# Attention with chosen places: who forms the sum of each head's 32 found values

## The chip, the cores and the metric

One Trainium2 chip, one of its cores. The metric is the device time of one execution in microseconds (us). Three runs of the kernel before gave 1508.18, 1509.52 and 1509.85; the median is 1509.52.

## The reference, cut to what matters

The model has four layers of gated cross-attention and feed-forward over 64 sequences of 64 tokens of 128 features. The change touches one sublayer, the attention of layer 1. It attends with only the 32 best of 64 context places for each token and head (4 heads of 32 features):

```
scores = einsum('bthd,bghd->bhtg', Q, K) / sqrt(DH)
topv, topi = top_k(scores, 32)
probs = softmax(topv)
attn = zeros_like(scores).at[bi, hi, ti, topi].set(probs)
attn_mean = attn.mean(axis=1)
c_t = einsum('btg,bgd->btd', attn_mean, x_vision @ Wv)
```

The result c_t gives scales and shifts (FiLM) for a state-space layer that comes after. The sum in the softmax runs over the 32 chosen places only.

## The kernel before

The 4096 tokens are 32 tiles of 128 tokens, tokens on partitions. The sublayer is `attention_ssm`. Each engine runs its own written list of steps, one step per tile (`pe_step`, `act_step`, `dve_step`, `pool_step`), and semaphores hold them together. The order in each step is written out by hand, and each queue is worked strictly in order. ScalarE and TensorE run their middle steps in a loop of two tiles each, VectorE and POOL only from tile 16 on.

**VectorE**, step t. For tiles 2 to 14 it first adds two tiles of the routed experts' rows, which POOL has gathered (`route.dve_pair`). Then it finds the 32 largest scores of each head in four rounds (`topk_round`): in each round four `max` (L1986) give the eight largest of each head, into `m8`, and four `match_replace` (L1992) overwrite them in the scores with the value TAKEN. After the first round it forms `nm`, the negative scaled maximum (L1995). Norm work for later tiles lies between the rounds. At the end it multiplies the exponentials `EX` with "was taken" (L2041), which zeroes the places that were not chosen, sums each head over its 64 places (L2043), and takes the reciprocal (L2045). The semaphore `tk` counts the halves of the rounds, 16 for each tile.

**ScalarE**, step t (`act_step`), in this order: scores of tile t+1 out of PSUM (L2161); values of t (L2170); `act_scale` of tile t-1, which waits for the reciprocal, masks it (L2151) and scales the four heads of EX (L2154); the norm's transpose and the keys of tile t+2 (L2175, L2133); the transposed attention of t-1 (L2179); the exponentials of tile t, 4 of 128x64 (L2182), which wait for `nm`; the context of t-1 (L2186); the query of t+2 (L2139); a norm of t+3 (L2146); the FiLM rows of t-1 (`act_film`, L2198 and L2199), which wait for TensorE's product.

**TensorE**, step t: scores of t+1 (L2270), values of t, transpose and keys of t+2, the bias row of the FiLM product of t-1 (L2291), then the transposed attention of t-1 (L2278, waits for act_scale), its context (L2286), the query of t+2 (L2262) and the FiLM product of t-1 (L2295, waits for L2186).

**POOL**, step t: the context mask onto the scores of t+1 (L1869), norm steps for later tiles, the modulation with the FiLM rows of t-1 (L1833, L1836), and in steps 0 to 12 the gathers of routed rows (L1316).

`thr_hits`, a scratch of 128 x 2 x 1032 bf16, belongs to another part of the kernel that counts weights above a threshold while layer 0 runs; in this sublayer it is free.

Of the kernel before, what the change touches and what calls it, by code (L numbers as in the profile page):

```python
# [11 lines left out]
ALU = mybir.AluOpType  # L12
ACT = mybir.ActivationFunctionType
AX = mybir.AxisListType
F32 = mybir.dt.float32
# [8 lines left out]
TILES = TOK // P  # L24
# [1682 lines left out]
def attention_ssm(k, io, freed, route):  # L1707


    nc = k.nc  # L1710
    H, DH, KTOP, GATE, HID = 4, 32, 32, 1, 4
    SCALE = float(DH) ** -0.5
    MASKED, TAKEN = -1e38, -3e38
    sem = lambda n, total=TILES: k.sem("a1_" + n, total)
# [4 lines left out]
    cv = Carve(k.arena)  # L1719
# [23 lines left out]
    W = cv.f32(2, H, CTX)  # L1743
    W2 = cv.f32(2, H, CTX)
    EX = cv.f32(2, H, CTX)
    m8 = cv.f32(4, H, 8)
    nm, sums, rec = cv.f32(2, H), cv.f32(2, H), cv.f32(2, H)
    vs = cv.f32(2, 2, D)
    aT = cv.f32(2, P)
# [13 lines left out]
    xt_full, xt_laid, q_full, q_laid, k_full, k_laid = (sem(n) for n in ("xT_full", "xT_laid", "q_full", "q_laid", "k_full", "k_laid"))  # L1763
    s_full, s_laid, s_masked, v_full, v_laid = (sem(n) for n in ("scores", "scores_laid", "masked", "v_full", "v_laid"))
    tk = sem("top", 16 * TILES)
    e_done, sel_done, n_step, a_done = sem("exp"), sem("selected"), sem("norm_step", 2 * TILES), sem("attn")
    r_done = sem("recip_masked")
    a_full, a_laid, c_full, cT_laid, f_full, f_laid = (sem(n) for n in ("attnT_full", "attnT_laid", "cT_full", "cT_laid", "film_full", "film_laid"))
    xs_step, xs_done = sem("xs_step"), sem("xs_done")

# [11 lines left out]
    def flat(v):  # L1782
        return v.rearrange("p h j -> p (h j)")

    def more(t, ahead):
        return not isinstance(t, int) or t + ahead < TILES
# [188 lines left out]
    def topk_round(e, t, s, r):  # L1975


        V = nc.vector
        src = W if r == 0 else W2
        before_round = 16 * t + 4 * r  # L1980
        for half in range(2):
            if r > 0:
                e.wait_ge(tk.sem, tk.at(before_round - 1 + half))
                e.nop(nofuse=True)
            for h in (2 * half, 2 * half + 1):
                ins = V.max(m8[:, r, h, :], src[:, s, h, :])  # L1986
            ins.then_inc(tk.sem, 1)
        for half in range(2):
            e.wait_ge(tk.sem, tk.at(before_round + 1 + half))
            e.nop(nofuse=True)  # L1990
            for h in (2 * half, 2 * half + 1):
                ins = V.match_replace(W2[:, s, h, :], m8[:, r, h, :], src[:, s, h, :], TAKEN)  # L1992
            ins.then_inc(tk.sem, 1)
        if r == 0:
            V.tensor_scalar(nm[:, s, :], m8[:, 0, :, 0], -SCALE, None, ALU.mult).then_inc(nm_done.sem, 1)  # L1995

    def norm_a(e, t, s):
        e.wait_ge(ln_rstd_done.sem, ln_rstd_done.at(t + 1))
        e.nop(nofuse=True)
        nc.vector.tensor_scalar(k.xn[:, s, 0, :], k.x[:, t, :], k.mv[:, 0, s, 0:1], k.rstd[:, 0, s:s + 1],  # L2000
                                ALU.subtract, ALU.mult).then_inc(ln_out_done.sem, 1)

    nm_done = sem("max_laid")

    def stats_a(e, t, s):
        nc.vector.bn_stats(k.stat[:, 0, s, :], k.x[:, t, :]).then_inc(ln_stats_done.sem, 1)

    def aggregate_a(e, t, s):
        e.wait_ge(ln_stats_done.sem, ln_stats_done.at(t + 1))
        e.nop(nofuse=True)  # L2010
        nc.vector.bn_aggr(k.mv[:, 0, s, :], k.stat[:, 0, s, :]).then_inc(ln_mv_done.sem, 1)

    def dve_step(e, t, s):

        V = nc.vector
        o = 1 - s
        if isinstance(t, int) and 2 <= t < 2 + route.PAIRS:
            route.dve_pair(e, t - 2)
        e.wait_ge(s_masked.sem, s_masked.at(t + 1))
        e.nop(nofuse=True)  # L2020
        topk_round(e, t, s, 0)
        if isinstance(t, int) and 2 <= t < 16:
            e.wait_ge(before.sem, min(route.AHEAD + 2 * t - 2, TILES))
            e.nop(nofuse=True)
        if more(t, 4):
            stats_a(e, t + 4, s)
        topk_round(e, t, s, 1)
        if more(t, 3):
            e.wait_ge(u_kept.sem, u_kept.at(t + 2))
            e.nop(nofuse=True)  # L2030
            e.wait_ge(xt_full.sem, xt_full.at(t + 2))
            e.wait_ge(b_out.sem, b_out.at(t + 2))
            norm_a(e, t + 3, o)
        topk_round(e, t, s, 2)
        if more(t, 4):
            aggregate_a(e, t + 4, s)
        topk_round(e, t, s, 3)
        e.wait_ge(e_done.sem, e_done.at(t + 1))
        e.wait_ge(tk.sem, tk.at(16 * t + 16))

        V.scalar_tensor_tensor(flat(EX[:, s, :, :]), flat(W2[:, s, :, :]), TAKEN, flat(EX[:, s, :, :]), ALU.is_equal, ALU.mult).then_inc(sel_done.sem, 1)  # L2041
        e.wait_ge(sel_done.sem, sel_done.at(t + 1))
        V.tensor_reduce(sums[:, s, :], EX[:, s, :, :], AX.X, ALU.add).then_inc(n_step.sem, 1)  # L2043
        e.wait_ge(n_step.sem, n_step.at(2 * t + 1))
        V.reciprocal(rec[:, s, :], sums[:, s, :]).then_inc(n_step.sem, 1)  # L2045

    def dve_first(e):
# [81 lines left out]
    def act_keys(e, t, s):  # L2129

        e.wait_ge(k_full.sem, k_full.at(t + 1))
        for h in range(H):
            last = nc.scalar.activation(kbd[:, s, :, h, :], ps[:, 2, 0:P].rearrange("p (b j) -> p b j", b=2), ACT.Copy,  # L2133
                                        scale=head_of[:, h:h + 1])
        last.then_inc(k_laid.sem, 1)

    def act_query(e, t, s):
        e.wait_ge(q_full.sem, q_full.at(t + 1))
        nc.scalar.copy(qT[:, s, :], ps[:, 1, 0:P]).then_inc(q_laid.sem, 1)  # L2139

    def act_norm_u(e, t, s):

        e.wait_ge(ln_out_done.sem, ln_out_done.at(t + 1))
        e.wait_ge(b_rstd.sem, b_rstd.at(t + 1))
        e.nop(nofuse=True)
        nc.scalar.activation(XS[:, t, :], k.xn[:, s, 0, :], ACT.Copy, scale=k.rstd[:, 1, s:s + 1]).then_inc(b_out.sem, 1)  # L2146

    def act_scale(e, t, s):

        e.wait_ge(n_step.sem, n_step.at(2 * t + 2))  # L2150
        nc.scalar.activation(rec[:, s, :], rec[:, s, :], ACT.Copy, scale=tmask[:, t:t + 1] if isinstance(t, int) else tmask[:, bass.ts(t, 1)]).then_inc(r_done.sem, 1)  # L2151
        e.wait_ge(r_done.sem, r_done.at(t + 1))
        for h in range(H):
            last = nc.scalar.activation(EX[:, s, h, :], EX[:, s, h, :], ACT.Copy, scale=rec[:, s, h:h + 1])  # L2154
        last.then_inc(a_done.sem, 1)

    def act_scores(e, t, s):
        e.wait_ge(s_full.sem, s_full.at(t + 1))
        if not (isinstance(t, int) and t < 2):
            e.wait_ge(tk.sem, tk.at(16 * t - 28))  # L2160
        nc.scalar.copy(flat(W[:, s, :, :]), ps[:, 3, 0:H * CTX]).then_inc(s_laid.sem, 1)  # L2161

    def act_step(e, t, s):

        o = 1 - s
        film = not (isinstance(t, int) and t == 0)
        if more(t, 1):
            act_scores(e, t + 1, o)
        e.wait_ge(v_full.sem, v_full.at(t + 1))
        nc.scalar.copy(vs[0:CTX, s, :, :].rearrange("p b d -> p (b d)"), ps[0:CTX, 4, 0:2 * D]).then_inc(v_laid.sem, 1)  # L2170
        if film:
            act_scale(e, t - 1, o)
        if more(t, 2):
            e.wait_ge(xt_full.sem, xt_full.at(t + 3))
            nc.scalar.copy(k.xnT[:, s, 0:P], ps[:, 0, 0:P]).then_inc(xt_laid.sem, 1)  # L2175
            act_keys(e, t + 2, s)
        if film:
            e.wait_ge(a_full.sem, a_full.at(t))
            nc.scalar.copy(aT[0:CTX, o, :], ps[0:CTX, 5, 0:P]).then_inc(a_laid.sem, 1)  # L2179
        e.wait_ge(nm_done.sem, nm_done.at(t + 1))  # L2180
        for h in range(H):
            last = nc.scalar.activation(EX[:, s, h, :], W[:, s, h, :], ACT.Exp, bias=nm[:, s, h:h + 1], scale=SCALE)  # L2182
        last.then_inc(e_done.sem, 1)
        if film:
            e.wait_ge(c_full.sem, c_full.at(t))
            nc.scalar.copy(cT[:, o, :], ps[:, 6, 0:P]).then_inc(cT_laid.sem, 1)  # L2186
        if more(t, 2):
            act_query(e, t + 2, s)
        if more(t, 3):
            act_norm_u(e, t + 3, o)  # L2190
        if film:
            act_film(e, t - 1, o)

    def act_film(e, t, s):
        e.wait_ge(xs_done.sem, xs_done.at(t))
        e.wait_ge(f_full.sem, f_full.at(t + 1))
        e.nop(nofuse=True)
        nc.scalar.copy(F[:, s, :], ps[:, 7, 0:2 * D])  # L2198
        nc.scalar.copy(FO[:, t, :], ps[:, 7, 2 * D:4 * D]).then_inc(f_laid.sem, 1)  # L2199
# [1147 lines left out]
```

## Time and profile before

| | us |
|---|---|
| median of three runs | 1509.52 |
| profiled execution, its own time | 1522.08 |
| span of its trace | 1520.4 |
| VectorE busy (share of the span) | 1090.0 (72%) |
| ScalarE busy | 922.1 (61%) |
| POOL busy | 687.8 (45%) |
| TensorE matmul busy | 1343.0 (88%) |
| this sublayer's tile loop | about 481 to 740 |

The profile is one execution, and its own time is above the median of the runs. A timeline row has the start, the duration (of all instructions merged in it), engine, line, operation, output and input, count, and in brackets the idle time of the engine before it with what ended it. "issue" is idle time for which the profile shows no cause. The granted clock of TensorE (PEclk) is a share of its full speed, 1.0.

### The profile page before, as it was taken

How to read it: one execution, taken by the hardware profiler on the slowest of the kernel's cores; microseconds unless marked ns; L12 is line 12 of the kernel's file. 1: busy time of each engine (PE TensorE's matmuls, PEld its weight loads, DVE VectorE, ACT ScalarE, POOL GpSimd, SP SyncE). 2: the span in 40 equal slices, each digit the busy share in tenths (PEclk: the TensorE clock that was granted, in tenths of full speed). 3: DMA queues.
4: the chain of work that ended last, by engine and by line, in shares of the span. 5: the costliest groups of instructions: out<-in, count | busy, mean ns of one | idle time of the engine just before them, and what ended most of it. 6: DMA issues, size and time to landing. Idle time of an engine off the chain costs nothing.

```text
span 1520.4 us, 49785 instructions
## 1 busy us (share of the span) xinstructions
PE 1343.0 (88%) x17625; PEld 1029.3 (68%) x17657; DVE 1090.0 (72%) x4573; ACT 922.1 (61%) x2012; POOL 687.8 (45%) x1336
## 2 busy tenths in 40 slices
PE   6999999999658688887789599988999999999998
PEld 5888888877545344444556366666877777788885
DVE  5878788877424799999868544436899899766664
ACT  5666665655335577787233355545688889865553
POOL 3655555576434688766166211113443343343331
PEclk9999999999875888899989799998999999999999
DMA  8050000001455401000020100000000000000000
GB/s 186 3 123 0 0 0 2 5 29 34 124 168 134 96 18 29 1 0 1 16 52 0 36 1 0 0 1 2 3 2 0 0 2 3 3 9 7 7 15 22
DMA packets 66868, 43.05 MB, mean 28 GB/s; under 512 B 24597, under 2 KB 63210, under 8 KB 66602
## 3 DMA queue, kind: packets, MB, share of 16 engines
q1 hardware_dynamic: 58346, 33.89, 9.1%
q0 software_dynamic: 2048, 4.20, 1.0%
q10 hardware_dynamic: 6336, 3.15, 0.7%
q8 instruction: 83, 1.36, 0.4%
q14 instruction: 55, 0.45, 0.1%
HBM read 28.64 MB, written 12.58 MB: 27 GB/s over the span
## 4 chain that ended last, share of the span: by engine, by line
PE 60%; DVE 18%; issue 8%; ACT 6%; POOL 5%; DMA 2%; DVEq 1%; SPq 0%; POOLq 0%; ACTq 0%
PE ps L775 4%; PE ps L344 4%; PE ps L784 4%; DVE arena L1992 4%; PE ps L386 4%; PE ps L337 4%; PE ps L366 3%; PE ps L2723 3%; DVE arena L1986 3%; PE ps L2730 3%; PE ps L377 3%; PE ps L2804 3%; PE ps L357 2%; PE ps L2717 2%; PE ps L2773 2%
## 5 line engine op out<-in xcount | busy, mean ns | idle before, releaser
L3236 POOL TENSOR_TENSOR arena<-arena 128x512 f32<-128x512 f32 x64 | 67.8, 1059 | 112.6 <-DVE arena L3160 112.6
L1992 DVE MATCH_REPLACE8 arena<-arena 128x64 f32<-128x64 f32 x512 | 101.8, 209 | 0.5 <-issue 0.2
L2482 DVE TENSOR_SCALAR_CACHE_REDUCE thr_hits<-thr_abs,thr_candidate 128x512 bf16<-128x512 f32 (+1 forms) x248 | 101.8, 477 | 0.0
L2723 PE MATMUL ps<-arena,toeplitz 96*128 96x128 f32 x512 | 71.5, 283 | 9.2 <-ACT arena L2955 4.0
L668 POOL TENSOR_TENSOR ln_veps<-ln_mv,eps 128x4 f32<-128x4 f32 x32 | 9.1, 284 | 154.5 <-DVE ln_mv L662 154.5
L1986 DVE MAX8 arena<-arena 128x8 f32<-128x64 f32 x512 | 75.9, 210 | 3.3 <-issue 2.0
L616 POOL TENSOR_TENSOR arena<-arena 128x1024 f32<-128x1024 f32 x32 | 61.4, 1918 | 34.8 <-DVE arena L557 34.8
L538 DVE TENSOR_REDUCE arena<-ps 128x16 f32<-128x1024 f32 x32 | 39.1, 1223 | 52.9 <-PE ps L357 52.8
L784 PEld LDWEIGHTS ps<-arena,toeplitz 128*128 128x128 f32 x512 | 63.5, 192 | 16.0 <-issue 13.3
L386 PEld LDWEIGHTS ps<-arena 128*64 128x64 f32 x1024 | 60.2, 139 | 19.8 <-issue 11.4
L2723 PEld LDWEIGHTS ps<-arena,toeplitz 96*128 96x128 f32 x512 | 63.0, 193 | 15.0 <-ACT arena L2955 9.8
L2717 PE MATMUL ps<-xnT,toeplitz 128*128 128x128 f32 x512 | 69.9, 281 | 3.2 <-ACT xnT L2894 3.2
L2804 PE MATMUL ps<-arena 128*64 128x128 f32 x1024 | 67.8, 273 | 3.1 <-ACT arena L2906 3.1
L2730 PE MATMUL ps<-toeplitz,arena 96*64 96x256 f32 x512 | 70.3, 396 | 0.0
L2804 PEld LDWEIGHTS ps<-arena 128*64 128x64 f32 x1024 | 59.9, 136 | 14.8 <-ACT arena L2906 7.0
L775 PE MATMUL ps<-xnT,arena 128*128 128x512 f32 x128 | 67.8, 622 | 0.0
L3134 DVE TENSOR_REDUCE arena<-ps 128x8 f32<-128x512 f32 x64 | 43.9, 685 | 33.4 <-PE ps L2792 33.3
L2278 PEld LDWEIGHTS ps<-ident,arena 128*64 128x64 f32 x256 | 28.0, 140 | 57.9 <-ACT arena L2154 56.4
L2717 PEld LDWEIGHTS ps<-xnT,toeplitz 128*128 128x128 f32 x512 | 63.8, 196 | 4.2 <-ACT xnT L2894 4.1
L386 PE MATMUL ps<-arena 128*64 128x128 f32 x1024 | 64.0, 277 | 2.1 <-ACT arena L457 2.1
L344 PE MATMUL ps<-xnT,arena 128*128 128x128 f32 x512 | 64.3, 280 | 1.6 <-DVE x_res L529 0.6
L784 PE MATMUL ps<-arena,toeplitz 128*128 128x128 f32 x512 | 64.9, 274 | 0.0
(463 smaller groups left out, 4157.2 us busy)
## 6 DMA issues: line engine op xcount, KB each, us to landing
toeplitz<-ssm_toeplitz_scratch SPq DMA_DIRECT2D x2, 2048.0 KB
arena<-L_ffn_packed SPq DMA_DIRECT2D x24, 128.5 KB, 3.2
toeplitz<-L_ffn_packed SPq DMA_DIRECT2D x24, 128.5 KB, 2.2
f_rows<-arena SPq DMA_DIRECT2D x2, 1536.0 KB, 9.5
f_outs<-arena ACTq DMA_DIRECT2D x12, 256.0 KB, 2.7
ssm_toeplitz_scratch<-ssm_padded_kernel SPq DMA_DIRECT2D x1, 2048.0 KB
out<-x_res SPq DMA_DIRECT2D x8, 256.0 KB, 2.3
arena<-ctx SPq DMA_DIRECT2D x2, 768.0 KB, 5.8
```

The lines of the kernel that those rows point to most:

```text
L344: last = nc.tensor.matmul(ps[:, 2 + c // 4, c % 4 * P:(c % 4 + 1) * P], w_q[:, c * P:(c + 1) * P], k.xnT[:, s, 0:P], start=True, stop=True)
L386: last = nc.tensor.matmul(ps[64 * b:64 * b + 64, 2, 0:D], OT[:, b, c, :], w_o[:, b, c, :], start=(c == 0), stop=(c == C - 1))
L775: nc.tensor.matmul(ps[:, u % 3, :], w1[:, x, c * P:(c + 1) * P], xnT, start=True, stop=True).then_inc(h_full.sem, 1)
L784: last = nc.tensor.matmul(ps[:, 3 + x % 2, j * P:(j + 1) * P], hT[:, u % 3, j * P:(j + 1) * P], w2[:, x, c, :], start=(c == 0 and j == 0), ...
L1986: ins = V.max(m8[:, r, h, :], src[:, s, h, :])
L1992: ins = V.match_replace(W2[:, s, h, :], m8[:, r, h, :], src[:, s, h, :], TAKEN)
L2482: ins = V.tensor_scalar(self.hits[:, j, at:at + n], self.abs[:, at:at + n], self.cand[:, c:c + 1].bitcast(F32), 0.0, ALU.is_ge, ALU.add, a ...
L2717: last = T_.matmul(ps[:, 1, c * P:(c + 1) * P], weights[phase].q[:, c * P:(c + 1) * P], xnT[:, s * P:(s + 1) * P], start=True, stop=True)
L2723: last = T_.matmul(ps[:, 0, c * P:(c + 1) * P], weights[phase].k[0:DC, c * P:(c + 1) * P], cg[0:DC, s, :], start=True, stop=True)
L2730: last = T_.matmul(ps[64 * m:64 * m + 64, 5, 256 * b:256 * b + 256], cg[0:DC, s, b * CTX:(b + 1) * CTX], by_parity[0:DC, m, :, :], start=T ...
L2804: last = T_.matmul(ps[64 * m:64 * m + 64, 0, 0:D], OT[:, m, c, :], w_o[:, m, c, :], start=(c == 0), stop=(c == C - 1))
L3236: G_.tensor_tensor(probs, probs, rc[:, s, :].unsqueeze(2).to_broadcast([P, heads, CTX]), ALU.mult).then_inc(s_prob.sem, 1)
```

## The change

The 32 found values of a tile stand in `m8` after the fourth search. Before, only the current tile's were kept, laid out by round. Now they are kept for two tiles in turn in `thr_hits`, so that each head's 32 values form a list. ScalarE takes the exponential of each head's list with an accumulated output, which is the head's sum (`act_sums`). It does so at the end of its step, after the FiLM rows, and waits for the fourth search's `max` only (`tk` at 14 of 16). VectorE drops its own sum and waits for ScalarE's before the reciprocal. `act_scale` waits for the selection by itself.

```diff
-    m8 = cv.f32(4, H, 8)
+    cv.at += 4 * H * 8
+    spare = k.thresholds.hits[:].rearrange("p a b -> p (a b)").bitcast(F32)
+    m8 = spare[:, 0:2 * H * 32].rearrange("p (s h r j) -> p s r h j", s=2, r=4, h=H)
+    top = spare[:, 256:256 + H * 32].rearrange("p (h j) -> p h j", h=H)
+    m8_list = spare[:, 0:2 * H * 32].rearrange("p (s h j) -> p s h j", s=2, h=H)
...
-                ins = V.max(m8[:, r, h, :], src[:, s, h, :])
+                ins = V.max(m8[:, s, r, h, :], src[:, s, h, :])
...
         V.scalar_tensor_tensor(flat(EX[:, s, :, :]), flat(W2[:, s, :, :]), TAKEN, flat(EX[:, s, :, :]), ALU.is_equal, ALU.mult).then_inc(sel_done.sem, 1)
-        e.wait_ge(sel_done.sem, sel_done.at(t + 1))
-        V.tensor_reduce(sums[:, s, :], EX[:, s, :, :], AX.X, ALU.add).then_inc(n_step.sem, 1)
-        e.wait_ge(n_step.sem, n_step.at(2 * t + 1))
+        e.wait_ge(sum_done.sem, sum_done.at(t + 1))
         V.reciprocal(rec[:, s, :], sums[:, s, :]).then_inc(n_step.sem, 1)
...
     def act_scale(e, t, s):
-        e.wait_ge(n_step.sem, n_step.at(2 * t + 2))
+        e.wait_ge(n_step.sem, n_step.at(t + 1))
...
         e.wait_ge(r_done.sem, r_done.at(t + 1))
+        e.wait_ge(sel_done.sem, sel_done.at(t + 1))
...
         if film:
             act_film(e, t - 1, o)
+        act_sums(e, t, s)
+
+    def act_sums(e, t, s):
+        e.wait_ge(tk.sem, tk.at(16 * t + 14))
+        for h in range(H):
+            last = nc.scalar.activation(top[:, h, :], m8_list[:, s, h, :], ACT.Exp, bias=nm[:, s, h:h + 1], scale=SCALE, accum_out=sums[:, s, h:h + 1])
+        last.then_inc(sum_done.sem, 1)
```

## Rows read from the trace of the kernel before

**Rows 1.** The chain of waits over 478 to 742 us, shares by line.

```profile
by line: DVE arena L1992 21.0%; DVE arena L1986 17.1%; issue 17.1%; DMA arena<-f_outs,arena 6.5%; DVE arena L2041 3.5%; DVE arena L2043 3.4%; POOL arena L1316 3.3%; POOL arena L1869 2.7%; POOL ln_rstd L1827 1.6%; POOL ln_rstd L1853 1.5%; PO
```

**Rows 2.** Windows: stretch, its length, each engine's busy us, granted clock, DMA share, GB/s.

```profile
560.00:600.00 40.00, 30.59 (x141) 17.89 (x139) 36.57 (x273) 29.05 (x108) 34.00 (x74) 0.88 0.06 16
...
640.00:680.00 40.00, 31.51 (x155) 17.60 (x153) 38.22 (x295) 32.01 (x120) 28.91 (x73) 0.96 0.00 0
```

**Rows 3.** Timeline of VectorE: the reciprocals of tiles 3, 14, 27 and 31.

```profile
522.02 0.18 DVE L2045 RECIPROCAL arena<-arena 128x4 f32<-128x4 f32 x1
...
611.20 0.18 DVE L2045 RECIPROCAL arena<-arena 128x4 f32<-128x4 f32 x1
...
706.61 0.18 DVE L2045 RECIPROCAL arena<-arena 128x4 f32<-128x4 f32 x1
...
733.65 0.18 DVE L2045 RECIPROCAL arena<-arena 128x4 f32<-128x4 f32 x1
```

**Rows 4.** Timeline of POOL: two starts of its step.

```profile
567.78 0.98 POOL L1869 TENSOR_TENSOR arena<-arena 128x256 f32<-128x256 f32 x1
...
576.18 0.98 POOL L1869 TENSOR_TENSOR arena<-arena 128x256 f32<-128x256 f32 x1
```

**Rows 5.** Timeline of ScalarE over one tile, from 626.89 us.

```profile
626.89 0.30 ACT L2151 ACTIVATE arena<-arena 128x4 f32<-128x4 f32 x1
...
629.63 1.07 ACT L2182 ACTIVATE arena<-arena 128x64 f32<-128x64 f32 x4
...
632.10 0.37 ACT L2198 COPY arena<-ps 128x256 f32<-128x256 f32 x1 [0.43 <-PE ps L2295]
632.37 0.38 ACT L2199 COPY arena<-ps 128x256 f32 x1
632.74 0.37 ACT L2161 COPY arena<-ps 128x256 f32<-128x256 f32 x1
...
633.34 0.30 ACT L2151 ACTIVATE arena<-arena 128x4 f32<-128x4 f32 x1
```

**Rows 6.** Timeline of VectorE at the end of a tile: fourth search, selection, reciprocal.

```profile
653.32 0.57 DVE L1986 MAX8 arena<-arena 128x8 f32<-128x64 f32 x4
...
654.70 0.42 DVE L2041 SCALAR_TENSOR_TENSOR arena<-arena 128x256 f32<-128x256 f32 x1
...
655.61 0.18 DVE L2045 RECIPROCAL arena<-arena 128x4 f32<-128x4 f32 x1
```

**Rows 7.** A line of VectorE in layer 0: count, duration min/median/max in ns.

```profile
L2482 DVE DVE_READ_ACCUMULATOR thr_hits<-thr_abs,thr_candidate x248: 75/84/90, 29.2 to 373.4; 128x1 f32 x124
```

**Rows 8.** ScalarE's groups by line and shape: busy us, mean ns of one, idle before.

```profile
L2182 ACT ACTIVATE arena<-arena 128x64 f32<-128x64 f32 x128 | 34.1, 339 | 8.4 <-DVE arena L1995 8.4
L2936 ACT ACTIVATE arena<-arena 128x512 f32<-128x512 f32 x64 | 40.4, 632 | 3.9 <-DVE arena L3138 2.7
L1229 ACT COPY arena<-ps 128x8 f32 x16 | 2.9, 183 | 0.0
```

**Rows 9.** Timeline of ScalarE: from act_scale to the first FiLM copy in three tiles.

```profile
545.30 0.30 ACT L2151 ACTIVATE arena<-arena 128x4 f32<-128x4 f32 x1
...
550.50 0.37 ACT L2198 COPY arena<-ps 128x256 f32<-128x256 f32 x1 [0.43 <-PE ps L2295]
...
594.39 0.30 ACT L2151 ACTIVATE arena<-arena 128x4 f32<-128x4 f32 x1 [2.01 <-DVE arena L2045]
...
600.77 0.37 ACT L2198 COPY arena<-ps 128x256 f32<-128x256 f32 x1 [1.03 <-PE ps L2295]
...
692.22 0.30 ACT L2151 ACTIVATE arena<-arena 128x4 f32<-128x4 f32 x1 [0.31 <-DVE arena L2045]
...
697.42 0.37 ACT L2198 COPY arena<-ps 128x256 f32<-128x256 f32 x1 [0.47 <-PE ps L2295]
```

**Rows 10.** Timeline of ScalarE in the last tiles.

```profile
727.45 0.30 ACT L2151 ACTIVATE arena<-arena 128x4 f32<-128x4 f32 x1 [0.47 <-DVE arena L2045]
...
732.93 0.38 ACT L2199 COPY arena<-ps 128x256 f32<-128x256 f32 x1
```

More of the change, by code:

```diff
@@ L1765, in attention_ssm @@
     tk = sem("top", 16 * TILES)
-    e_done, sel_done, n_step, a_done = sem("exp"), sem("selected"), sem("norm_step", 2 * TILES), sem("attn")
-    r_done = sem("recip_masked")
+    e_done, sel_done, n_step, a_done = sem("exp"), sem("selected"), sem("recip"), sem("attn")
+    r_done, sum_done = sem("recip_masked"), sem("top_sums")
     a_full, a_laid, c_full, cT_laid, f_full, f_laid = (sem(n) for n in ("attnT_full", "attnT_laid", "cT_full", "cT_laid", "film_full", "film_laid"))
@@ L1991, in topk_round @@
             for h in (2 * half, 2 * half + 1):
-                ins = V.match_replace(W2[:, s, h, :], m8[:, r, h, :], src[:, s, h, :], TAKEN)
+                ins = V.match_replace(W2[:, s, h, :], m8[:, s, r, h, :], src[:, s, h, :], TAKEN)
             ins.then_inc(tk.sem, 1)
         if r == 0:
-            V.tensor_scalar(nm[:, s, :], m8[:, 0, :, 0], -SCALE, None, ALU.mult).then_inc(nm_done.sem, 1)
+            V.tensor_scalar(nm[:, s, :], m8[:, s, 0, :, 0], -SCALE, None, ALU.mult).then_inc(nm_done.sem, 1)
     def norm_a(e, t, s):
```

## The prediction, made before the result was known

> **What bounds the kernel now.** I went first to the chain of waits over the stretch in which the attention with chosen places runs, 478 to 742 us. There the reader sees that VectorE carries most of it: the match-and-replace line 21.0%, the search for the eight largest 17.1%, the selection 3.5% and the row sum 3.4%, with some POOL lines behind [rows 1]. Then the windows: at 640 to 680 VectorE is busy 38.22 of 40 us, ScalarE 32.01, POOL 28.91; at 560 to 600 VectorE 36.57, POOL 34.00, ScalarE 29.05 [rows 2]. By shares ScalarE has about 8 us in 40 to spare. The timelines decide where that room lies.
>
> The starts of the reciprocal, one per tile, give the pace. Tile 3 is at 522.02, tile 14 at 611.20, tile 27 at 706.61 and tile 31, the last, at 733.65 [rows 3]. That is 8.11 us a tile for 11 tiles, 7.34 for 13 and 6.76 for 4. In the first of these POOL, which also gathers the routed rows, goes round in 8.40 us (576.18 less 567.78) without waiting [rows 4], and late in the stretch VectorE is held to it. From tile 15 on VectorE sets the pace alone.
>
> Now ScalarE. From 626.89 to 633.34 it was behind and waited for no reciprocal: one whole tile takes it 6.45 us [rows 5]. Of these, 5.21 pass from the masking of the reciprocal (L2151) to the first film copy (L2198), 0.64 on the two film copies, and 0.60 on the scores and values copies (L2161, L2170). It is 6.45 and not less because the queue waits inside it for TensorE, which waits for ScalarE's own earlier results (the 0.43 at L2198). So the queue's own round is 6.45 us against 7.34, a slack of 0.89 and not the 1.5 that the shares suggest.
>
> **The change part by part.** VectorE loses the row sum. From the start of the selection to that of the reciprocal are 0.91 us (655.61 less 654.70), of which the selection is 0.42 and 0.03 for the handover [rows 6]; the sum with its own handover is the other 0.46. All of it lies on VectorE's own path, so with nothing else it would be worth 0.46 in each tile that VectorE paces. Which memory holds the list, and the stride, change no instruction's count; I cost them at nothing, by the same size of operand. The moved wait for the selection in act_scale costs nothing either: the selection ends before the sums do, below.
>
> ScalarE gains four exponentials of 128x32 with an accumulated output, last in its step, behind the film copies. Call their time in the queue S. Four exponentials of 128x64 take 1.07 us [rows 5], and one of them 339 ns [rows 8], so they start (1.07 - 0.34)/3 = 0.24 apart. Half the columns are worth little: (632 - 339)/448 is 0.65 ns a column, 0.02 for 32, which leaves 0.22 each and 0.87 for four. The accumulated output on ScalarE stands nowhere in this trace. On VectorE it is an instruction of its own, DVE_READ_ACCUMULATOR, 84 ns [rows 7]. I bound it from below by nothing (S = 0.87), from above by a full loss of the overlap and a read as long as ScalarE's own shortest copy: 0.32 + 0.18 = 0.50 each [rows 8], S = 2.0. A gain below 0.87 is excluded, since the four are added whole and nothing leaves this queue. I take half the overlap lost and a read like VectorE's, the one row of such a read: 0.22 + 0.05 + 0.08 = 0.35, S = 1.4.
>
> The Trainium skill (ScalarE: Activation LUTs, Rules for kernel authors) budgets about 0.3 us for an ACTIVATE with a pointer bias and 0.83 ns an element, by which S would be 1.3. For four of 64 columns it gives 1.4 where the trace shows 1.07; the trace decides for plain ones, and for accumulating ones no row speaks. By the rule the sum below would be some 3 us smaller.
>
> What is queued behind decides. The reciprocal of tile t now waits for sums(t). Sums(t) stand behind film(t-1), and that stands behind act_scale(t-1), which waits for the reciprocal of t-1. So a ring closes that was open before: reciprocal, mask and scale, TensorE's transposes, the copy, exponentials of tile t, context, film product, film copies, sums, reciprocal. After the sums ScalarE does the scores and values copies (0.60), and under them the reciprocal (0.18 [rows 6]) is done. The ring's period is 6.45 + S. VectorE waits in it: its fourth search ends at 653.89 [rows 6], 6.1 us behind the reciprocal before it, and sums begin 6.45 behind it (0.60 + 5.21 + 0.64), so the wait on the search costs nothing and the sums end after the selection in every tile.
>
> Third, TensorE. The 5.21 is at full clock. Over the seven tiles whose L2151 starts at 545.30 to 594.39 the same way takes 5.20, 6.15, 5.20, 7.40, 5.21, 5.21 and 6.38: the last is 600.77 less 594.39 [rows 9]. That is 0.61 over 5.21 in the mean, in a stretch with TensorE busy 30.59 of 40 us and a granted clock of 0.88, both of its levels by turns; for the ten from 626.89 to 692.22 it is 0.09 (one at 0.85), at a clock of 0.96 [rows 2, 5, 9]. Call it K. Before, K hardly cost anything, for the reciprocal set the next start; in the ring it counts in full. The new ring idles TensorE by S more in each tile, like the first stretch; I take K = 0.45, nearer to it, bounds 0.09 and 0.61.
>
> The period is then 6.45 + 1.4 + 0.45 = 8.30. POOL's 8.40 of the first stretch is hardly touched: it is ahead of VectorE there and waits for nothing. But VectorE ran at less than that up to tile 8 and built up the lead that it lost later, and now it goes at 8.30 from tile 3 on. From tile 3 to 27: 24 x 8.30 = 199.2 against 184.6, +14.6. For the last four tiles keys, queries and scores fall away and TensorE fills the gaps: 727.45 to 732.93 is 5.48, plus 0.37 (633.34's tile, 632.37 to 632.74) is 5.85 to the sums [rows 5, 10]; then S, the reciprocal with two handovers 0.33, and K of 0.2 since these tiles all ran at full clock: 7.78 x 4 = 31.1 against 27.0, +4.1. Tiles 0 to 2 are hidden: VectorE waits there for gathered rows, and the film copies on which those hang come ahead of the added work. What follows the loop is untouched.
>
> Sum: +18.7 us. On the profiled execution, 1522.08 us (span 1520.4 and 1.7 around it), this is 1540.8. The median of the runs is 12.6 us below that execution; I carry the difference over: 1528.2 us.
>
> At the low ends (S 0.87, K 0.09) the period is 7.41: POOL still hides the first 11 tiles, 13 x 7.41 is +0.9, the tail +1.2: +2, 1511.6. At the high ends (2.0, 0.61) it is 9.06: 217.4 - 184.6 = +32.8, and the tail is 4 x 8.79 less 27.0 = +8.1: +41, 1550.5.
>
> **The rivals.** First, the sums are hidden and the row sum's time comes back. Mechanism: ScalarE gets to the sums before VectorE's selection ends, so the reciprocal waits for nothing. For it speaks ScalarE's idle time, 2.01 us in front of a single L2151 [rows 9]. Against it: that idle time lies in front of act_scale, behind the reciprocal, and the ring has none of it. It decides where 6.45 + S + K is under VectorE's new round of 7.34 - 0.46 = 6.88, thus S + K under 0.43, or if the queue's round is shorter than I read. It would give 0.46 x 17 tiles (15 to 31) = -7.8: 1501.7 us. Chance 0.07.
>
> Second, the ring closes but S and K are at their low ends and POOL covers the early tiles: +0 to +3, 1511 us. Chance 0.10.
>
> Third, a read of the accumulator that stops the queue, and a TensorE that falls to its lower level in every tile, K about 1 instead of by turns. With S at 1.7: 9.15 x 24 = 219.6, +35.0, and the tail 4 x 8.88 less 27.0 = +8.5: 1553. For it speaks the 7.40 in the middle of the first stretch; against it that four of its seven tiles were at full clock. Chance 0.15.
>
> **How the numbers follow.** My forecast, between +4 and +30, has the remaining 0.68; its time, 1528.2, is the predicted one. The range for 8 in 10 runs from the low ends to just under the third rival's sum: 1511 to 1547. A difference of over 0.2%, 3 us, is about what a measurement of this kernel tells from none. Faster takes the first rival, 0.07. Within it lies most of the second, 0.09. Slower is the rest, 0.84.
>
> **What would show it.** In the profile after, TENSOR_REDUCE is gone from the loop and the reciprocal is preceded by idle VectorE time of 1 us or more, ended by ScalarE's exponentials; ScalarE no longer waits for the reciprocal in front of act_scale, only for TensorE; the reciprocals are 8.3 us apart from tile 3 to 27 and 7.8 in the last four. The exponentials of 128x32 with their reads show S directly: 1.4 us for four. The granted clock between 600 and 720 falls from 0.96 toward 0.88. It would be wrong if the reciprocal follows the selection without idle time (first rival), or if the period is right while S and K are not: then the ring is right and its terms are mis-sized.

## The result and the profile after

The changed kernel took 1516.84 us (median of 7 runs, 1514.09 to 1522.02) against 1509.85 for the kernel before beside it (7 runs): ratio 1.0046, 95% interval 1.0027 to 1.0066, so +6.9 us with 4 to 10. Slower, as forecast, but by little more than a third of the +18.7.

The two profiled executions stand the other way round: 1514.1 us of span against 1520.4. That difference lies ahead of this sublayer. Part of it can be seen: in the execution of before, TensorE stood still once for 13.59 us in the routed experts of layer 0, on its timeline:

```profile
427.42 1.86 PE L1360 MATMUL ps<-arena 128*128 128x128 f32 x7 [13.59 <-issue]
```

The changed kernel's execution has no such gap there; its longest between 400 and 480 us is 7.99 us, and it reaches tile 3 fourteen us earlier. The gap is of the execution and not of the change: e2 and e10 below are one and the same kernel and show 14.71 and 7.03 us. So I count from the reciprocal of tile 3 to the end of the span: 1520.4 - 522.0 = 998.4 before, 1514.1 - 507.9 = 1006.2 after, +7.8, which agrees with the runs. The reciprocals that answer to [rows 3], from VectorE's timeline of the changed kernel:

```profile
507.93 0.18 DVE L2047 RECIPROCAL arena<-arena 128x4 f32<-128x4 f32 x1 [0.57 <-ACT thr_hits L2201]
...
595.42 0.18 DVE L2047 RECIPROCAL arena<-arena 128x4 f32<-128x4 f32 x1 [0.45 <-ACT thr_hits L2201]
...
695.38 0.18 DVE L2047 RECIPROCAL arena<-arena 128x4 f32<-128x4 f32 x1 [0.94 <-ACT thr_hits L2201]
...
726.07 0.18 DVE L2047 RECIPROCAL arena<-arena 128x4 f32<-128x4 f32 x1 [1.40 <-ACT thr_hits L2201]
```

| us | tiles 3 to 14 (11) | 14 to 27 (13) | 27 to 31 (4) | sum |
|---|---|---|---|---|
| before | 89.2 | 95.4 | 27.0 | 211.6 |
| after | 87.5 | 100.0 | 30.7 | 218.1 |
| forecast for after | 91.3 | 107.9 | 31.1 | 230.3 |

Of the 32 reciprocals 27, and all from tile 14 on, now have idle VectorE time in front of them, ended by ScalarE's exponentials. From the waits of VectorE over 478 to 740 us (total, times, longest), and the windows that answer to [rows 2]:

```profile
DVE arena L2047 <- ACT thr_hits L2201: 25.2, 27, 2.2
```

```profile
560.00:600.00 40.00, 30.86 (x146) 17.14 (x145) 35.52 (x283) 34.23 (x150) 34.35 (x77) 0.91 0.11 27
640.00:680.00 40.00, 31.40 (x149) 17.38 (x147) 33.37 (x274) 35.26 (x158) 27.04 (x70) 0.92 0.00 0
```

At 640 to 680 VectorE fell from 38.2 to 33.4 busy us and ScalarE rose from 32.0 to 35.3. One tile of ScalarE, from its timeline; it answers to [rows 5] and shows the new work (L2201), with the second and third head left out:

```profile
626.73 0.31 ACT L2153 ACTIVATE arena<-arena 128x4 f32<-128x4 f32 x1
...
631.94 0.37 ACT L2208 COPY arena<-ps 128x256 f32<-128x256 f32 x1 [0.42 <-PE ps L2305]
632.21 0.38 ACT L2209 COPY arena<-ps 128x256 f32 x1
632.47 0.33 ACT L2201 ACTIVATE thr_hits<-thr_hits,arena 128x32 f32<-128x32 f32 x1
632.70 0.20 ACT L2201 ACTIVATION_READ_ACCUMULATOR thr_hits<-thr_hits,arena 128x1 f32 x1
...
633.40 0.31 ACT L2201 ACTIVATE thr_hits<-thr_hits,arena 128x32 f32<-128x32 f32 x1
633.61 0.19 ACT L2201 ACTIVATION_READ_ACCUMULATOR thr_hits<-thr_hits,arena 128x1 f32 x1
633.70 0.36 ACT L2164 COPY arena<-ps 128x256 f32<-128x256 f32 x1
633.95 0.37 ACT L2173 COPY arena<-ps 64x256 f32<-64x256 f32 x1
634.22 0.31 ACT L2153 ACTIVATE arena<-arena 128x4 f32<-128x4 f32 x1
```

The way from L2153 to L2208 is still 5.21 us. S is 1.23 (632.47 to 633.70), and the whole tile 7.49. On VectorE, the selection ends at 632.92 and the reciprocal follows 0.93 us later, which answers to [rows 6]:

```profile
632.49 0.43 DVE L2045 SCALAR_TENSOR_TENSOR arena<-arena 128x256 f32<-128x256 f32 x1
633.84 0.18 DVE L2047 RECIPROCAL arena<-arena 128x4 f32<-128x4 f32 x1 [0.93 <-ACT thr_hits L2201]
```

Most tiles are 7.49 us apart. About every third or fourth takes 8.3 to 8.5, and in these TensorE's FiLM product takes 2.08 us where it takes 1.13 in the next tile, at a mean granted clock of 0.80 against 1.00: for part of the tile TensorE is at the lower of its two levels, 1.2 GHz, and for the rest at 2.4. ScalarE's timeline, TensorE's, and windows over the two tiles:

```profile
618.28 0.31 ACT L2153 ACTIVATE arena<-arena 128x4 f32<-128x4 f32 x1
...
624.45 0.37 ACT L2208 COPY arena<-ps 128x256 f32<-128x256 f32 x1 [1.32 <-PE ps L2305]
```

```profile
619.74 1.09 PE L2288 MATMUL ps<-ident,arena 128*64 128x128 f32 x8 [1.46 <-ACT arena L2157]
...
622.29 2.08 PE L2305 MATMUL ps<-arena 128*128 128x512 f32 x2
...
630.73 1.13 PE L2305 MATMUL ps<-arena 128*128 128x512 f32 x2
```

```profile
618.30:624.50 6.20, 4.37 (x18) 2.36 (x20) 5.99 (x52) 4.62 (x20) 3.61 (x10) 0.80 0.00 0
626.70:632.00 5.30, 3.94 (x20) 2.15 (x20) 5.30 (x48) 4.67 (x20) 3.03 (x8) 1.00 0.00 0
```

### The profile page after: what moved, and what is told of

Read it like the earlier page. It is cut to its first block, busy times and chain, and to the rows that moved or that the text cites. A ratio compares the mean times of both kernels' runs of the same rounds, so it can differ in the third digit from the quotient of the medians.

```text
span 1514.1 us, 50106 instructions
## 1 busy us (share of the span) xinstructions
PE 1331.0 (88%) x17657; PEld 1019.0 (67%) x17657; DVE 1073.0 (71%) x4541; ACT 953.6 (63%) x2268; POOL 687.7 (45%) x1336
## 4 chain that ended last, share of the span: by engine, by line
PE 34%; DVE 7%; ACT 5%; issue 3%; POOL 2%; DVEq 0%; ACTq 0%; POOLq 0%
PE ps L775 4%; PE ps L784 4%; PE ps L2733 3%; PE ps L2740 3%; PE ps L2814 3%; PE ps L2727 2%; PE ps L2783 2%; PE ps L2794 2%; PE ps L2886 2%; PE ps L2802 2%; PE ps L2855 1%; PE ps L2372 1%; PE ps L2395 1%; PE ps L2388 1%; POOL ln_rstd L670 1%
## 5 line engine op out<-in xcount | busy, mean ns | idle before, releaser
L1996 DVE MATCH_REPLACE8 arena<-thr_hits,arena 128x64 f32<-128x64 f32 x512 | 101.4, 208 | 0.0
L1990 DVE MAX8 thr_hits<-arena 128x8 f32<-128x64 f32 x512 | 75.7, 208 | 2.9 <-issue 1.9
L2288 PE MATMUL ps<-ident,arena 128*64 128x128 f32 x256 | 35.6, 283 | 39.8 <-ACT arena L2157 39.8
L2814 PE MATMUL ps<-arena 128*64 128x128 f32 x1024 | 67.8, 273 | 3.1 <-ACT arena L2916 3.1
L337 PE MATMUL ps<-arena 96*128 96x128 f32 x512 | 65.2, 281 | 0.0
```

The lines of the kernel that those rows point to most:

```text
L337: last = nc.tensor.matmul(ps[:, c // 4, c % 4 * P:(c % 4 + 1) * P], w_k[0:DC, c * P:(c + 1) * P], cg[0:DC, s, :], start=True, stop=True)
L1990: ins = V.max(m8[:, s, r, h, :], src[:, s, h, :])
L1996: ins = V.match_replace(W2[:, s, h, :], m8[:, s, r, h, :], src[:, s, h, :], TAKEN)
L2288: last = T.matmul(ps[0:CTX, 5, 0:P], EX[:, s, h, :], k.ident[:], start=(h == 0), stop=(h == H - 1))
L2814: last = T_.matmul(ps[64 * m:64 * m + 64, 0, 0:D], OT[:, m, c, :], w_o[:, m, c, :], start=(c == 0), stop=(c == C - 1))
```

## The experiments

Ten runs, each in five rounds against the kernel before on the same chip; e6 repeats the changed kernel and e10 repeats e2. The stretches are from one profiled execution each, as in the table above. "us" is the ratio less 1, times the median of before.

| kernel | ratio, interval | us | 3 to 14 | 14 to 27 | 27 to 31 |
|---|---|---|---|---|---|
| e1 sums unused, VectorE's sum kept | 1.0076, 1.0053 to 1.0099 | +11.6 | 89.1 | 99.4 | 30.6 |
| e2 sums ahead of the FiLM rows | 0.9981, 0.9964 to 0.9998 | -2.9 | 88.2 | 93.9 | 25.8 |
| e3 no sums at all | 0.9947, 0.9924 to 0.9969 | -8.1 | 88.4 | 87.8 | 25.3 |
| e4 filler of 384 columns | 1.0055, 1.0032 to 1.0078 | +8.4 | 88.2 | 101.1 | 30.4 |
| e5 no accumulated output | 1.0025, 1.0007 to 1.0044 | +3.8 | 87.7 | 96.0 | 30.8 |
| e6 changed kernel again | 1.0048, 1.0026 to 1.0069 | +7.3 | 87.7 | 102.5 | 30.7 |
| e7 e2 and the mask on VectorE | 1.0022, 1.0003 to 1.0041 | +3.3 | 89.1 | 96.6 | 26.4 |
| e8 filler of 640 columns | 1.0054, 1.0035 to 1.0073 | +8.2 | 87.6 | 97.5 | 29.8 |
| e9 e2 with the wait in halves | 0.9971, 0.9951 to 0.9991 | -4.4 | 88.1 | 91.8 | 25.5 |
| e10 e2 again | 0.9980, 0.9965 to 0.9995 | -3.0 | 88.6 | 92.3 | 25.8 |

The theory in the expectations: the time was lost because ScalarE's round of one tile became longer than VectorE's (queue theory). Its rival: it was lost because VectorE stands still for the sums (wait theory).

**e1.** Onto the changed kernel:

```diff
-        e.wait_ge(sum_done.sem, sum_done.at(t + 1))
+        e.wait_ge(sel_done.sem, sel_done.at(t + 1))
+        V.tensor_reduce(sums[:, s, :], EX[:, s, :, :], AX.X, ALU.add).then_inc(n_step.sem, 1)
+        e.wait_ge(n_step.sem, n_step.at(2 * t + 1))
         V.reciprocal(rec[:, s, :], sums[:, s, :]).then_inc(n_step.sem, 1)
...
-... accum_out=sums[:, s, h:h + 1])
+... accum_out=other[:, s, h:h + 1])
```

VectorE also waits at a step's start until the sums of two tiles before are done, since they read the same buffer; they are long done by then.

> ScalarE does its four accumulating exponentials as in the changed kernel, but their result goes to a tile that nobody reads; VectorE keeps its own row sum and never waits for them. Queue theory (the cost is that ScalarE's round of one tile, 6.26 us and the 1.23 us of the sums, is longer than the 7.34 us at which VectorE went): the wait of VectorE does not matter, so tiles 7.49 us apart with a jump now and then, and +5 to +8 us against before, like the changed kernel. Wait theory (the cost comes from VectorE standing still for the sums): the time of before, within 2 us.

Measured: +11.6 us, 99.4 in the 13 tiles. VectorE needs nothing of the new work and is held all the same, now in front of its selection, because the tile's own exponentials of 64 columns (L2189 here) come late from the same queue. Its timeline:

```profile
649.79 0.43 DVE L2047 SCALAR_TENSOR_TENSOR arena<-arena 128x256 f32<-128x256 f32 x1 [1.01 <-ACT arena L2189]
...
657.29 0.43 DVE L2047 SCALAR_TENSOR_TENSOR arena<-arena 128x256 f32<-128x256 f32 x1 [0.39 <-ACT arena L2189]
```

The wait theory falls. The idle time in front of the changed kernel's reciprocal is where the queue's length shows, not its cause. The size was outside the 5 to 8 us that I expected. The loop from tile 3 to 31 took 219.0 us, 7.4 more than before, as the queue theory has it. Another 3.3 come behind it: at the last reciprocal ScalarE still has its sums ahead of it, act_scale starts 2.22 us behind it (0.22 before), and the last tile's FiLM rows start 9.61 us behind it (6.28 before). The other 1.3 are TensorE's products at its lower level, as in the changed kernel.

**e2.**

```diff
+        act_sums(e, t, s)
         if film:
             act_film(e, t - 1, o)
-        act_sums(e, t, s)
```

> The changed kernel with the sums ahead of the FiLM rows in ScalarE's step. Queue theory with its order: the 0.42 us in which ScalarE waits for TensorE's FiLM product are now filled, so its round falls from 7.49 to about 7.1 and VectorE, at 6.88 in the mean, is nearly the pace: 1 to 5 us under before. If only the amount of work on ScalarE counts and not its place: the time of the changed kernel, +5 to +8.

Measured: -2.9 us, and 9.8 less than the changed kernel by the ratios. Nothing was taken away, only moved. The sums fill the time in which ScalarE waited for TensorE, so the FiLM copy has no idle time before it, and the tile is 6.96 us (ScalarE's timeline, 652.69 to 659.65). A second thing changes with the order: only one of the 13 tiles is a long one, at 8.01, where the changed kernel had three; the shorter tile is the larger part of the gain (13 times 7.49 less 7.13 is 4.7 of 6.1 us).

```profile
652.69 0.31 ACT L2153 ACTIVATE arena<-arena 128x4 f32<-128x4 f32 x1
...
657.08 0.40 ACT L2148 ACTIVATE arena<-xn,ln_rstd 128x128 f32 x1
657.39 0.30 ACT L2201 ACTIVATE thr_hits<-thr_hits,arena 128x32 f32<-128x32 f32 x1
...
658.61 0.35 ACT L2208 COPY arena<-ps 128x256 f32<-128x256 f32 x1
...
659.65 0.31 ACT L2153 ACTIVATE arena<-arena 128x4 f32<-128x4 f32 x1
```

**e3.** The four exponentials are replaced by one copy; the sums are left out and the result is not the attention's.

```diff
-        for h in range(H):
-            last = nc.scalar.activation(top[:, h, :], ..., accum_out=sums[:, s, h:h + 1])
-        last.then_inc(sum_done.sem, 1)
+        nc.scalar.copy(sums[:, s, :], k.onesq[:, 0:H]).then_inc(sum_done.sem, 1)
```

> Leaves the sums out: one ScalarE copy of 128x4 constants stands in their place, everything else as in the changed kernel. It shows what dropping VectorE's row sum is worth when ScalarE has no work for it. Queue theory: ScalarE's round is 6.26 and 0.2, VectorE paces at about 6.88: -5 to -8 us against before. If VectorE's row sum was not on the path: no gain.

Measured: -8.1 us, at the edge of the 5 to 8 expected. Tiles are 6.50 and 6.95 us apart by turns, and in most the reciprocal follows the selection with no wait (VectorE's timeline). This is what dropping the row sum is worth where ScalarE's share is free:

```profile
656.99 0.42 DVE L2045 SCALAR_TENSOR_TENSOR arena<-arena 128x256 f32<-128x256 f32 x1
657.33 0.17 DVE L2047 RECIPROCAL arena<-arena 128x4 f32<-128x4 f32 x1
657.42 0.58 DVE L1990 MAX8 thr_hits<-arena 128x8 f32<-128x64 f32 x4
...
663.83 0.17 DVE L2047 RECIPROCAL arena<-arena 128x4 f32<-128x4 f32 x1
...
670.78 0.17 DVE L2047 RECIPROCAL arena<-arena 128x4 f32<-128x4 f32 x1
```

**e4 and e8.** TensorE's wait for act_scale filled with unused products; e8's text is this, e4 has the first of the two only.

```diff
             pe_film_bias(e, t - 1)
+            for width in (BANK - P, 2 * P):
+                T.matmul(ps[:, 6, P:P + width], k.ident[:], wf[:, 0:width], start=True, stop=True)
             pe_attn(e, t - 1, o)
```

> The changed kernel with one more TensorE product (128x384, result unused) ahead of the transposed attention of each tile, where TensorE waits for ScalarE. Clock theory (tiles of 8.4 instead of 7.49 us are those where TensorE fell to its lower level in that wait): the long tiles go, 2 to 5 us less than the changed kernel, +2 to +5 against before. If the long tiles come from something else: the time of the changed kernel or more, and 8.4 us tiles stay.

> The changed kernel with TensorE's wait for act_scale filled by 640 columns of unused products instead of 384 as in e4. If the fall of the granted clock in every third or fourth tile comes from TensorE's idle time in that wait, it goes now or becomes rarer. If it does not depend on that idle time, tiles of 8.4 us stay as often as in e4, and the time is that of e4.

Measured: with 384 columns the long tiles stayed (four of 8.3 to 8.5 between tiles 14 and 27) and the time was that of the changed kernel, a miss. With 640 columns they are gone: all 13 tiles are 7.49 to 7.54 apart, and the granted clock at 640 to 680 is 1.00 against 0.92. The windows of e4 and of e8:

```profile
640.00:680.00 40.00, 34.57 (x158) 19.36 (x157) 33.67 (x276) 35.10 (x156) 27.06 (x71) 0.92 0.00 0
```

```profile
640.00:680.00 40.00, 35.95 (x179) 21.30 (x178) 36.20 (x294) 36.28 (x158) 26.16 (x68) 1.00 0.00 0
```

TensorE's wait for act_scale shows what the filler left of it. Outside the tiles next to a long one it is 1.46 us in the changed kernel and in e6 (three and four long tiles in the 13), 0.81 in e4 (four), 0.71 in e2 and e10 (one and none) and 0.38 in e8 (none). From TensorE's timelines of e4, e10 and e8:

```profile
659.03 1.09 PE L2288 MATMUL ps<-ident,arena 128*64 128x128 f32 x8 [0.81 <-ACT arena L2157]
```

```profile
657.18 1.09 PE L2288 MATMUL ps<-ident,arena 128*64 128x128 f32 x8 [0.71 <-ACT arena L2157]
```

```profile
653.03 1.09 PE L2288 MATMUL ps<-ident,arena 128*64 128x128 f32 x8 [0.38 <-ACT arena L2157]
```

So the long tiles come from TensorE's idle time, as far as one execution of each kernel shows it. But e8's runs did not become faster than e6's beside them (+8.2 and +7.3, intervals overlapping), though its 13 tiles took 5.0 us less than e6's in the profiled executions. The profiled execution of e8 was the fastest of its runs (1510.99 against a median of 1517.48) and that of e6 the slowest of its own (1522.38 against 1519.13), so these two may not stand for the rest; what the long tiles cost the runs is not shown. Part of it is that e8's last stretch, from ScalarE's first copy behind the convolution to the end of the span, was 765.4 us against 762.8. The executions fall into two groups there: before, after, e1, e6 and e10 at 762.8 to 763.2, e2, e3, e4, e5, e7, e8 and e9 at 765.4 to 767.2. Since e2 (766.0) and e10 (763.0) are the same kernel, the group belongs to the execution and not to the kernel.

**e5.** The four exponentials without their accumulated output, then the copy of e3; the result is not the attention's.

> The changed kernel with the four exponentials kept and the accumulated output left out; the sums are a 128x4 copy of constants, so the result is not the attention's. It splits S. If the accumulator's read costs queue time (starts 0.31 us apart with it against 0.22 without, as the traces show): 4 x 0.09 less and about 0.15 to 0.2 more for the copy, so tiles 7.3 us apart instead of 7.49, about 3 us under the changed kernel. If the read is free: the changed kernel's tile and 0.15 us more.

Measured: +3.8, 3.5 less than e6 beside it, with intervals that overlap; tiles are 7.22 us apart where TensorE's clock does not fall. ScalarE's timeline, four exponentials merged:

```profile
640.78 0.96 ACT L2201 ACTIVATE thr_hits<-thr_hits,arena 128x32 f32<-128x32 f32 x4
641.64 0.18 ACT L2202 COPY arena<-ones_square 128x4 f32<-128x4 f32 x1
```

Without the read four take 0.86 us of the queue (640.78 to 641.64), with it 1.23: the read costs 0.09 each, though it lasts 0.19, because it overlaps its neighbours.

**e6.** The changed kernel again.

> The changed kernel itself, on the chip and beside the kernels of this call. +5 to +10 us against before, the tile loop as in its first profile: 7.49 us a tile, with a long tile now and then.

Measured: +7.3 us. Its 13 tiles took 102.5 against 100.0, with three of 8.4 and one of 9.73 among them where the first had three: that much differs from execution to execution.

**e7.** On top of e2:

```diff
-        V.reciprocal(rec[:, s, :], sums[:, s, :]).then_inc(n_step.sem, 1)
+        V.reciprocal(rec[:, s, :], sums[:, s, :]).then_inc(r_done.sem, 1)
+        e.wait_ge(r_done.sem, r_done.at(t + 1))
+        V.tensor_scalar(rec[:, s, :], rec[:, s, :], tmask[...], None, ALU.mult).then_inc(n_step.sem, 1)
...
-        nc.scalar.activation(rec[:, s, :], rec[:, s, :], ACT.Copy, scale=tmask[...]).then_inc(r_done.sem, 1)
```

> The sums ahead of the FiLM rows as in e2, and the masking of the reciprocal (a 128x4 multiply) moved from ScalarE to VectorE. Queue theory: ScalarE's round falls by 0.33 to about 6.75, VectorE's rises by 0.2 to about 6.9 in the mean, and the pace is the longer: 6.9 against 7.13 in e2 and 7.34 before, thus 5 to 8 us under before. If a handover between two small operations on VectorE costs what ScalarE saves: the time of e2, 2 to 3 us under before.

Measured: +3.3, a miss on both sides. Tiles alternate between 7.11 and 7.84: VectorE paces again, above the 7.13 of e2, and ScalarE now waits for its fourth search (9.4 us in 12 tiles between 600 and 700). Against e3, whose short tile is 6.50, two things are added, on VectorE's timeline. The small multiply starts 0.34 us behind the reciprocal, and the next search 0.47 behind it where e3 has 0.09, so the multiply costs 0.38 instead of the 0.2 that I gave it. And the reciprocal starts 0.59 us behind the selection where e3 has 0.34, because the sums cannot start before the fourth search and end after the selection; that 0.25 my expectation did not have. Together they make 6.50 into 7.11; in the long tiles, 6.95 in e3, another 0.28 is left open.

```profile
645.04 0.18 DVE L2047 RECIPROCAL arena<-arena 128x4 f32<-128x4 f32 x1 [0.16 <-ACT thr_hits L2201]
...
645.51 0.60 DVE L1990 MAX8 thr_hits<-arena 128x8 f32<-128x64 f32 x4
...
651.55 0.43 DVE L2045 SCALAR_TENSOR_TENSOR arena<-arena 128x256 f32<-128x256 f32 x1
652.14 0.18 DVE L2047 RECIPROCAL arena<-arena 128x4 f32<-128x4 f32 x1 [0.16 <-ACT thr_hits L2201]
652.48 0.23 DVE L2049 TENSOR_SCALAR arena<-arena 128x4 f32<-128x4 f32 x1 [0.16 <-DVE arena L2047]
```

**e9 and e10.** e10 is e2. e9 is e2 with

```diff
-        e.wait_ge(tk.sem, tk.at(16 * t + 14))
         for h in range(H):
+            if h % 2 == 0:
+                e.wait_ge(tk.sem, tk.at(16 * t + 13 + h // 2))
```

> The order of e2 (sums ahead of the FiLM rows), and the sums of heads 0 and 1 wait only for the first half of the fourth search, those of heads 2 and 3 for the second. In e2 ScalarE stood 0.28 us for the search in every second tile and VectorE 0.16 us for the sums. If that handover is what holds e2 at 7.13 us a tile: about 7.0, 1 to 2 us under e2. If ScalarE's own work of 7.0 us is: the time of e2, 2 to 5 us under before.

> The kernel of e2 once more, to see whether its gain stands on another chip and day: 1 to 5 us under before, and 8 to 12 under the changed kernel.

Measured: e10 -3.0, e9 -4.4 us. Both have the whole computation and both beat the kernel before; by the ratios, on different chips, e10 is also 10.3 us under e6. e9's tiles are 6.95 and 7.05 by turns, with one of 8.03, against 6.96 and 7.31. The two intervals overlap: that e9 is better than e2 rests on its tiles in one execution, and the runs do not show it.

## Why the prediction missed

The direction and the mechanism held: the sums stand behind the FiLM rows, ScalarE's round exceeds the pace of VectorE, the reciprocal gets idle time before it. But the forecast's sum was 2.7 times the measured one, and the step that failed is "The period is then 6.45 + 1.4 + 0.45 = 8.30". All three terms were too large.

**S, taken at 1.4, is 1.23.** I had taken the read at 84 ns and half the overlap as lost. The read adds 0.09 each and the overlap of the exponentials stays: e5's four start 0.215 apart, close to the 0.22 that I had worked out from the plain ones. The estimate of 1.3 by the rule of the Trainium skill (ScalarE: Activation LUTs, Rules for kernel authors) came nearer here. The rule counts neither the overlap, 0.11 us an exponential against e5's starts, nor the read, 0.09, and the two nearly cancel.

**The queue's own round, read as 6.45, is 6.26.** In [rows 5] 0.37 us lie between the second film copy and the scores copy; in the changed kernel it is 0.26 to the first exponential, and the scores and values copies are 0.25 apart instead of 0.33. In the kernel before, these two copies stood right behind the products of TensorE that they wait for, on TensorE's timeline:

```profile
631.95 0.65 PE L2270 MATMUL ps<-arena 128*64 128x256 f32 x4
632.44 0.60 PE L2307 MATMUL ps<-arena 128*64 128x128 f32 x4
```

The scores product ends at 632.60 and its copy starts at 632.74, the values product at 633.04 and its copy at 633.07. In the changed kernel the same products end at 632.44 and 632.88, and the copies start at 633.70 and 633.95, so that wait is over before they come up. I had taken every start-to-start distance in a tile without a listed wait as work of the queue. The 0.19 are read from the two timelines; no run isolates them.

**K, taken at 0.45, is 0.20 in these 13 tiles** (99.96/13 = 7.69 less 7.49) and 0.39 in e6. I had taken it near the stretch with the same idle time of TensorE. That TensorE's clock falls with its idle time agrees with e8; how often it would strike was not to be had from the trace of before.

Together the period is 7.7 to 7.9 and no longer 8.3, and that turns a second sentence: "now it goes at 8.30 from tile 3 on". Under about 8.1 POOL hides the first eleven tiles. It still goes round in 8.4 late in the stretch (577.93 less 569.52, to be set against [rows 4]):

```profile
569.52 0.97 POOL L1873 TENSOR_TENSOR arena<-arena 128x256 f32<-128x256 f32 x1
577.93 0.98 POOL L1873 TENSOR_TENSOR arena<-arena 128x256 f32<-128x256 f32 x1
```

The changed kernel and all ten others, even e3, have 87.5 to 89.1 there. So what I put down as +2.1 was -1.7; the 13 tiles gave +4.6 against +12.5, and the last four +3.6 against +4.1. The last stretch held best because its terms were read from tiles of its own kind. The 1.3 us between +6.5 in the loop and +7.8 to the end are the last tile's FiLM rows, 7.55 us behind the last reciprocal against 6.28: TensorE was at its lower level there (granted clock 0.53 over 727.7 to 729.7, in the kernel before 1.00 over the same product) and took 1.90 us for the transposed attention instead of 1.09. The forecast had nothing for it.

My bound at the low ends, +2, and the second rival came closer than the forecast: the ring closed, POOL covered the early tiles, and only K and a part of S were above their low ends. The stated range of 1511 to 1547 held the 1516.8, but near its low end; the forecast of +18.7 lies far outside the measured 4 to 10.

The first rival was wrong as the kernel stands, but its price was right: e3 shows -8.1 us where I had -7.8. And its condition, that ScalarE gets to the sums in time, could be met in part by order alone, as e2 and e9 show with -2.9 and -4.4 of the -8.1; I had worked out the 0.43 us wait for TensorE inside the round and did not ask what would happen if the new work filled it.

## What to carry to other kernels

An engine's spare time is not its idle share but the difference between its own round, with the waits that it closes through another engine, and the pace. New work at the end of such a round lengthens it in full (here by 1.23 us, of which 1.08 were slack). The same work put where the engine waits for another's answer lengthens it less, by the wait that it fills (here 0.42 us, for the FiLM product), which was enough to come under the pace of 7.34; so look for that wait first and place the work ahead of it. When a sum has several terms that each were taken between wide ends, ask at which value another limit takes over (here POOL's 8.1 us), for on either side of it the same error costs very different amounts.

## What was not expected of the hardware

- A read of ScalarE's accumulator is an instruction of its own, 186 to 203 ns over 128 of them, and costs 0.09 us of queue time behind an exponential of 32 columns (e5 against the changed kernel).
- The same gap of TensorE in every tile did not lower its clock in every tile but in one of three or four, and the long tiles came three or four tiles apart; e4's filler left that as it was, and in e8's profiled execution there was none (0.92 and 1.00 in the windows above).
- A 128x4 multiply that reads what the instruction before it on VectorE wrote started 0.34 us behind it, of which 0.16 idle, through its semaphore.
